# A five-stage software pipeline on one core: the order in which each engine walks through the groups in flight

## The reference

```
x = x + tanh(g_xattn[0]) * performer(layernorm(x), ctx, ctx)      # 16 heads of 8, 32 random features,
                                                                 # exp features, causal running sums S, Z; out = num / den
x = x + tanh(g_ffn[0])   * channel_mix(layernorm(x))              # xr, xk = mu*x + (1-mu)*x_prev
                                                                 # sigmoid(xr@W_r) * (relu(xk@W_k)**2 @ W_v)
x = x + tanh(g_xattn[1]) * gated_attention(ctx, layernorm(x))     # queries of x, keys and values of ctx; two softmaxes:
                                                                 # a = softmax(qk); w*softmax(gate*a) + (1-w)*a; @v @w_proj
x = x + tanh(g_ffn[1])   * quantised_ffn(layernorm(x))            # 8-bit activations, ternary weights,
                                                                 # silu(gate)*up, inner 512, then down
```

## Time and profile before

| | |
|---|---|
| median of 3 runs | 619.16 us |
| the profiled execution | 618.45 us, of which its span is 616.7 us |
| PE busy | 486.8 us (79%), 7446 matmuls |
| PE weight loads (PEld) | 360.5 us (58%) |
| DVE busy | 452.3 us (73%) |
| ACT busy | 365.4 us (59%) |
| POOL busy | 346.7 us (56%) |
| mean granted clock of PE | 0.906 |

### The profile page before, as it was taken

How to read it: one execution, slowest core, us unless ns; L and a number is a source line. 1 busy time by engine, 2 the same in 40 slices (tenths; PEclk the granted TensorE clock), 3 DMA queues, 4 the chain that set the end, 5 groups by cost and what they waited for, 6 DMA issues and landing times.

```text
span 616.7 us, 18941 instructions
## 1 busy us (share of the span) xinstructions
PE 486.8 (79%) x7446; PEld 360.5 (58%) x7476; DVE 452.3 (73%) x1353; ACT 365.4 (59%) x747; POOL 346.7 (56%) x476
## 2 busy tenths in 40 slices
PE   0357799999898888797969896988799898877652
PEld 0235567676766665666757674857476666564541
DVE  2443357888888888688868979698968887767643
ACT  2231347667677767576656766767657676554432
POOL 5013248667676767566656675666647666644420
PEclk9999999989899999798969798899979898868655
DMA  7300000000001000101010101010100100000000
GB/s 212 62 1 11 18 20 10 28 2 15 25 10 29 11 27 12 28 2 35 3 36 3 35 2 37 2 28 10 33 5 2 36 2 11 1 11 2 10 9 9
DMA packets 24863, 13.01 MB, mean 21 GB/s; under 512 B 2257, under 2 KB 24657, under 8 KB 24785
## 3 DMA queue, kind: packets, MB, share of 16 engines
q1 hardware_dynamic: 22288, 10.69, 6.5%
q10 hardware_dynamic: 2496, 1.14, 0.7%
HBM read 9.73 MB, written 2.10 MB: 19 GB/s over the span
## 4 chain that ended last, share of the span: by engine, by line
PE 57%; DVE 22%; issue 10%; ACT 6%; SPq 2%; DMA 1%; POOL 1%; DVEq 0%; ACTq 0%; POOLq 0%
PE MC L1425 11%; PE TP L1391 7%; PE FP L1301 6%; PE MA L1317 6%; PE SP L1382 3%; PE SP L1490 2%; DVE mx L958 2%; DVE SL L964 2%; DVE gmean L893 2%; PE FP L1281 2%; PE FP L1251 2%; PE SP L1368 2%; PE MA L1339 2%; PE MA L1349 2%; PE FP L1285 1%
## 5 line engine op out<-in xcount | busy, mean ns | idle before, releaser
L1425 PE MATMUL MC<-Vc,ET 128*64 128x25 f32 x2048 | 73.7, 221 | 10.5 <-DVE X L1076 8.2
L1425 PEld LDWEIGHTS MC<-Vc,ET 128*64 128x64 f32 x2048 | 68.1, 142 | 23.7 <-issue 22.2
L394 POOL TENSOR_TENSOR Zn<-Zn,Gs 128x1024 f32<-128x1024 f32 x32 | 60.9, 1902 | 23.9 <-DVE Gs L988 23.7
L918 DVE TENSOR_TENSOR WT<-FP,mask 128x512 f32<-128x512 f32 x64 | 42.2, 682 | 37.5 <-PE FP L1301 37.5
L386 POOL TENSOR_TENSOR Zn<-E,rsh 128x1024 f32<-128x1024 f32 x32 | 60.9, 1903 | 13.4 <-DVE rsh L978 12.3
L355 POOL TENSOR_SCALAR ft<-ft 128x512 f32<-128x512 f32 x64 | 39.7, 620 | 48.0 <-ACT ft L552 44.2
L362 POOL TENSOR_SCALAR kX<-kT,bm 128x256 f32<-128x256 f32 x128 | 59.6, 482 | 4.0 <-ACT kT L530 4.0
L599 ACT ACTIVATE ET<-TP 128x512 f32<-128x512 f32 x64 | 36.6, 596 | 29.0 <-PE TP L1391 28.7
L1391 PE MATMUL TP<-ident,E 128*128 128x128 f32 x256 | 48.3, 321 | 2.6 <-ACT E L588 2.4
L1301 PE MATMUL FP<-ft 32*64 32x64 f32 x2048 | 40.4, 231 | 2.9 <-POOL ft L355 2.9
L1301 PEld LDWEIGHTS FP<-ft 32*64 32x64 f32 x2048 | 35.8, 143 | 11.5 <-issue 11.4
(11 more groups left out here) (192 smaller groups left out, 1266.0 us busy)
## 6 DMA issues: line engine op xcount, KB each, us to landing
Cd<-in_ctx SPq DMA_DIRECT2D x32, 128.0 KB, 3.0
call<-in_ctx SPq DMA_DIRECT2D x4, 512.0 KB, 8.9
X<-in_x SPq DMA_DIRECT2D x16, 128.0 KB, 3.0
out_x<-X SPq DMA_DIRECT2D x16, 128.0 KB, 2.2
wffn<-in_L_ffn_w_gate ACTq DMA_DIRECT2D x1, 256.0 KB, 8.7
wffn<-in_L_ffn_w_up ACTq DMA_DIRECT2D x1, 256.0 KB, 8.5
wffn<-in_L_ffn_w_down ACTq DMA_DIRECT2D x1, 256.0 KB, 9.0
wkv<-in_L_xattn_w_kv ACTq DMA_DIRECT2D x1, 128.0 KB, 7.1
```

Source lines behind the costliest of these rows:

```text
L394: pool.tensor_tensor(z, z, Gs[u][:, :].unsqueeze(2).to_broadcast([P, H, 64]), ALU.mult).then_inc(s("zn"), 1)
L918: v.tensor_tensor(WT[u][:, b, :, :], FP[:, 512 * b:512 * b + 512].rearrange("p (c l) -> p c l", l=64), mask[:, :].unsqueeze(1).to_broadcas ...
L1425: last = mm(MC[64 * j:64 * j + 64, c + 32 * q:c + 32 * q + 25], weights[:, q, 64 * j:64 * j + 64], Vc[g.p][:, 2 * u + j, q, 0:25], start=T ...
```

## The change

The order in which the four engines' `step` lists its functions changes, and with it where `features(g, 1)`, `ftp(g, 1)`, `weights0(g, 0)`, `causal(g, 0)`, `causal(g, 1)` (from place b to a), `token_mix`, `ffn0_in`, `relu_k`, `tanh_r` (from c to b), `quant_clip`, `quant_rec`, `quant_mul` (from e to d) are done, and `gates_mean` (from a to b), `scaled(g, 0)`, `gated(g, 0)`, `gated_G(g, 0)`, `outA(g, 0)` (from c to d). The waits in the functions are set anew to fit. No operation, tile or bank is added or taken away. SP's order is as it was. The new orders in full, halves behind a point:

The diff at the places of which the working speaks (PE's front and end, DVE's front and end, one wait):

```diff
             def step(a, b, c, d, e):                       # PE
-                if b:
-                    features(b, 1)
                 if d:
                     turn1(d, 2)
-                if c:
-                    ffn0_in(c)
+                    outA(d, 0)
+                    turn1(d, 3)
+                if b:
+                    weights0(b, 1)
+                if c:
+                    ffn0_out(c)
...
+                if a:
+                    weights0(a, 0)
+                if b:
+                    ffn0_in(b)
                 if e:
                     ffn_dn(e, 1)
-                if b:
-                    rows_BT(b)
-                if c:
-                    outA(c, 0)
...
             def step(a, b, c, d, e):                       # DVE
-                if e:
-                    quant_clip(e)
-                    quant_rec(e)
-                if c:
-                    token_mix(c)
+                if d:
+                    gated(d, 0)
+                    gated_G(d, 0)
                 if e:
                     quant_kh(e)
-                if d:
+                if b:
+                    gates_mean(b)
+                if d:
+                    first(d, 0)
                     least(d, 1)
...
-                if a:
-                    gates_mean(a)
+                if a:
+                    causal(a, 0)
+                    causal(a, 1)
...
             def weights0(g, u):
...
                 elif u == 1:
-                    at(pe, s("Vc"), g.k * 2 + 2)
-                    gate_at(pe, s("kT"), g.k + 1, s("pe_passed"))
+                    gate_at(pe, s("WT"), g.k * 4 + 2, s("pe_passed"))
```

More of the change, by code:

```diff
@@ L414, in step @@
                     quant_int(e)
-                if b:
-                    ftp(b, 1)
                 if d:
-                    shifted(d, 1)
+                    scaled(d, 0)
                 if c:
@@ L421, in step @@
                 if d:
+                    shifted(d, 1)
                     scaled(d, 1)
@@ L1177, in step @@
                     veD(d)
-                if c:
-                    least(c, 0)
                 if b:
-                    nbB(b)
-                if e:
-                    ffn_out(e, 0)
-                if c:
-                    shift(c, 0)
+                    gates_Tb(b)
                 if a:
@@ L1189, in step @@
                     largest(c, 1)
+                if e:
+                    ffn_out(e, 0)
                 if d:
                     nbD(d)
+                if c:
+                    less(c, 1)
+                if b:
+                    token_mix(b)
+                if c:
+                    least(c, 0)
+                if d:
+                    quant_max(d)
+                if c:
+                    shift(c, 0)
+                if d:
+                    quant_clip(d)
+                    quant_rec(d)
                 if e:
                     ffn_out(e, 1)
-                if c:
-                    less(c, 1)
-                    gated(c, 0)
-                    gated_G(c, 0)
-                if d:
-                    quant_max(d)
                 if a:
-                    gates_mean(a)
+                    causal(a, 0)
+                    causal(a, 1)
             run(v, step, late)
@@ L1528, in step @@
                 if d:
-                    turn1(d, 3)
+                    outA(d, 1)
                 if e:
@@ L1533, in step @@
                     turn2(d, 0)
-                if c:
-                    ffn0_out(c)
+                if b:
+                    out0(b, 0)
                 if d:
-                    outA(d, 1)
                     turn2(d, 1)
                 if b:
-                    weights0(b, 0)
-                if c:
-                    gates_bc(c)
+                    out0(b, 1)
+                if d:
+                    outB(d, 0)
                 if e:
@@ L1545, in step @@
                 if d:
-                    outB(d, 0)
                     turn2(d, 2)
@@ L1554, in step @@
                     rows_CT(c)
-                if b:
-                    out0(b, 0)
-                if c:
+                    gates_bc(c)
                     queries(c)
-                if b:
-                    weights0(b, 1)
+                if a:
+                    rows_T(a)
                 if c:
```

239 lines of the change are left out of this document (120 added, 119 removed).

## The result

| | before | after |
|---|---|---|
| median | 618.79 us, 4 runs (617.78 to 619.92) | 600.07 us, 4 runs (592.04 to 601.78) |
| ratio, with its 95% interval | 1 | 0.9624 [0.9523, 0.9724] |
| the profiled execution | 618.45 us, span 616.7 | 599.03 us, span 597.2 |

The changed kernel is faster, and 600.07 us lies inside the range. The ratio compares undisturbed executions only, so it is lower than the quotient of the two medians.

What follows compares the result with a forecast made beforehand. It took PE and DVE waiting for each other in turn as the bound. Span 616.7 - 21.8 (middle) + 8 (fill) - 16 (drain) = 586.9 us, given as 590 us measured; range 574 to 614.

Steps and rivals of the forecast that it cites:

- The bound: Clean step of 30.78 us: PE and DVE wait for each other; perfect order wins 3.5 us at most, to DVE's 27.2.
- 1, the front: Front of a step: PE's three waits (1.5 for xM, 0.5 and 0.5 us) lose their cause as work moves earlier.
- 2, the step: DVE through the whole step: 29.0 us a step, ends 27.5 and 31; twelve steps 348.0 without the loop's ends.
- A: Rival, chance 0.13: ve_C on DVE also waits for POOL's `scaled`, +1.8 us a step, +22 in all: 612.
- B: Rival, 0.15 with its like: POOL's `shifted` locks out `gated_G(d,1)` and `quant_clip`; about 3.8 us net a step, +53: 643.
- C: Rival, chance 0.10: gmean gets ahead of the lock, DVE saves 1.6 us, step about 27.7: 574.
- D: Rival, chance 0.07: no gain, the stalls only change places, middle as before: 611 to 619.
- The 0.5 us for nb_A: DVE in the step: nb_A leaves `with_bias` as its neighbour, beside which it takes 0.68: minus 0.5 us.
- 3, the loop's end: PE's stall stays and DVE loses 4.6: 4.8 us each, 19.2 for four, ends 3.4 and 6.5; middle -21.8.
- 4, the fill: Pipeline fill: `late()` 11 us later, step 1 about 4 shorter, steps 2 and 3 about even; net +8, ends 0 and +13.
- 5, the drain: Pipeline drain: group's work ends one step earlier in three places; 90.5 instead of 106.1 us, -16, ends -5 and -20.

Runs made afterwards that it cites:

- the block put back: Kernel after with `token_mix`, `ffn0_in`, `relu_k` and `tanh_r` back at the next step's front: 601.98 us, ratio 0.9704 [0.9638, 0.9769].

## Why the prediction was right, and where its sizes were off

The account of the step held in its parts. The forecast span was 10 us too short, since the loop's end was priced too low; it would have been 15 too short had the fill not been priced too high.

**The bound.** That the step is set by PE and DVE waiting for each other, and can fall to little above DVE's busy time, held: DVE is busy 93% of the clean step, and PE's waits fell from 4 to 2.4 us.

**1, the front.** The xM wait is gone, and the other two at the front with it. The reason was half right: putting the block back brings the wait back in the fill (2.27 us), not in the step.

**2, the step.** 29.0 forecast, 28.76 in the clean step and 28.7 to 29.1 in the others. `outA(d,1)` waits 0.62 for `first` (0.5 forecast), the end of the step 1.02 for ACT's E (0.9). gmean 1.87, Gs and amc 0.17, ve_C 0.23 say that rivals A, B and C did not occur, as the gain says of D, and moving gmean shows that its length comes from the neighbour: beside no 1.9 us POOL operation it takes 0.29. The rule of the Trainium skill ("SBUF — State Buffer", Who interferes with whom) that the two engines lock each other out for a whole instruction agrees with these rows: gmean and `scaled` ended within 0.01 us of each other, at 480.94 and 480.93. The 0.5 us for nb_A came as forecast (0.68 to 0.14), though Gs, with which it was compared, is 128 x 16 and nb_A 128 x 2.

**3, the loop's end: the term that was mis-sized.** 4.8 us each forecast, in this profile (379.9 - 12 x 28.8) / 4 = 8.6, and 6.8 where no long stretch of low clock falls in. The first stall was right (2.97 to 3.50 us, where the earlier trace rows have 3.4 at most), and that DVE stands behind it. Not foreseen was the second pause of 0.93 to 2.21 us, in the middle of the `outA` for which DVE waits: `gated` starts 8.3 us after the stall's begin (248.97 - 240.70) where I had 6.2. Before, there is one stall only the earlier trace rows: `outA(c,0)` then stood ahead of the jump and DVE stood idle later instead (5.25 us ahead of vr). The middle is thereby -9.2 instead of -21.8: +15.1 from the ends, -2.4 from the steps. Of the 15.1, 7.9 are the one long stretch of low clock, for which the sum had no term; without it an end cost 6.8, just outside the 3.4 to 6.5 that were given.

**4, the fill.** +3.7 forecast as +8. `late()` ended where I put it: its last transposes start at 50.24, `weights0(b,1)` at 51.63. PE's first instruction behind it comes 12.3 us later than before (51.63 against 39.37). The next three steps, from PE's first instruction of one to that of the next, took 27.0, 29.0 and 26.1 us before and 24.4, 21.2 and 28.1 after: -2.7 where 4 were forecast, then -7.8 and +1.9 where both were called about even. The term that failed is thus the third step (m = 2), from 29.0 to 21.2. Products of PE there, in the timeline of the kernel after:

```profile
72.06 1.99 PE L1302 MATMUL FP<-ft 32*64 32x64 f32 x64 [2.35 <-POOL ft L355]
...
95.12 1.16 PE L1302 MATMUL FP<-ft 32*64 32x64 f32 x64 [1.74 <-POOL ft L355]
```

The same 64 products take 1.99 us at 72.06 and 1.16 at 95.12; in the kernel before they still took 1.93 at 83.17. The change from the long form to the short comes at about 78 us after, 2 us into that step, and at about 85 before, 19 us into it. This fits the record of the granted clock, which begins at 77.4 and 84.9. Why PE speeds up earlier in the new order no run tests; the block put back moves it to about 99.

**5, the drain.** 90.5 forecast, 92.1 measured. The parts are less good than the sum: step 16 took 27.5 us (27 forecast), step 17 26.4 (24), `project` of the last group stood at 14.9 in step 18 (17.5), and behind it came 23.3 us (22 forecast for a chain that took 23.2 before, a cut for which the sum gives no reason). Two misses of 2.5 cancel, and that is luck. Without loop's ends the stretch from `project_T` of group 12 on fell less, from 111.8 to 101.9 us, and with them from 117.1 to 103.2, of which 3.4 go with the block of part 1.

**The total.** The forecast of 590 stood against 600.07 with a profile at 599.03, and against 596.56 with one at 592.72. The errors by stretch: middle +12.6 (of which 7.9 is the one long stretch at low clock), fill -4.3, drain +2.0 against the rounded -16: together 10.3, and 597.2 - 586.9 = 10.3.

**What stays open.** Whether PE waits for its instructions in the stall and in the second pause, as the times of the packets suggest, isn't tested: no run changes their loading by itself. Open too is why the granted clock stays low behind one loop's end for 6 us and behind another for over 20, in the same program.

## What to carry to other kernels

A reordering is worth what its steady step gains, less what it puts behind the points where an engine stands still anyway: at a loop's jump, price the stall, what stands behind it and the granted clock after it together. Shortening one of them alone, DVE's idle time from 6 to 3.8 us or the stall to 2.6, gave no gain that could be told. Write out a short loop once and compare, before tuning inside it: here 37 us of order became 19.5 to 26 with the loop, and an edit that won 0.7 us a step showed only once the loop was gone. In a full step a wait that is removed tends to reappear at the next input; sum the waits of the whole step before claiming one.

## What the runs showed of the hardware that I had not expected

A jump back in PE's loop costs 2.6 to 4.5 us of standing still, the least where `weights0` follows it and the most where `outA` does, and in one arrangement a second pause of 0.9 to 2.4 us after 21 of 32 products (with the block put back after 27, in three of four). With `outA(d,1)` or `weights0(b,1)` right behind the jump there is one stall only. All of them end 1.3 to 2.1 us behind the end of a 16 KB packet of the queue "instruction". The low clock behind it is worth as much as the stall: intervals of 30.5 and of 38.1 us came from stalls of 2.59 and 2.67. In the fill the granted clock reads 0.98 over all of its 98.9 us, while the same 64 products first take 1.99 us and then 1.16. The record of the clock begins only at 77.4 us, just where the products get short (at 84.9 in the kernel before, at 99.2 with the block put back), and the views print 1.00 for the time ahead of it: there the row of the clock doesn't tell how fast PE runs, and the time of one known instruction does.
